# Experts' outputs summed in DRAM by accumulating indirect transfers, and the scatter stage's gate and residual moved into the distance projections

## The reference

```python
g, m = jax.lax.top_k(probs.transpose(0, 2, 1), k)      # k = 128 tokens for each expert
xin = x[batch_idx, m]
h = jax.nn.gelu(jnp.einsum('nekd,edf->nekf', xin, w1), approximate=False)
h = jnp.einsum('nekf,efd->nekd', h, w2)
out = jnp.zeros((n, t, d)).at[batch_idx, m].add(g[..., None] * h)
...
x = x + s * silu(out)                                   # end of the third layer
xn = layernorm(x)                                       # the fourth begins
```

## Time and profile before

| | us |
|---|---|
| three runs, median (lowest to highest) | 3836.95 (3835.36 to 3840.81) |
| the profiled execution | 3840.4 |
| its span | 3838.3 |
| PE busy | 3246.2 (85%) |
| DVE busy | 3057.9 (80%) |
| ACT busy | 2302.0 (60%) |
| POOL busy | 1711.6 (45%) |

### The profile page before, as it was taken

How to read it: one execution, slowest core, us unless ns; L and a number is a source line. 1 busy time by engine, 2 the same in 40 slices (tenths; PEclk the granted TensorE clock), 3 DMA queues, 4 the chain that set the end, 5 groups by cost and what they waited for, 6 DMA issues and landing times. The chain is left out here.

```text
span 3838.3 us, 56660 instructions
## 1 busy us (share of the span) xinstructions
PE 3246.2 (85%) x16737; PEld 1730.1 (45%) x16737; DVE 3057.9 (80%) x4922; ACT 2302.0 (60%) x2769; POOL 1711.6 (45%) x851
## 2 busy tenths in 40 slices
PE   7767988889897997868799999899986977877776
PEld 3322333333236885645434344599985741121111
DVE  6879999999996776856588988577776768888887
ACT  4766666666763334634366666322222759999998
POOL 0009998989983111012200000111134338989996
PEclk9878999999998998977789999999998987888888
DMA  3542333332312356847822333222123642334432
GB/s 126 198 186 118 132 143 144 144 131 108 144 47 92 122 142 167 215 98 243 248 53 77 71 77 75 73 66 66 52 66 111 188 143 95 122 117 126 126 118 83
DMA packets 300300, 465.56 MB, mean 121 GB/s; under 512 B 49687, under 2 KB 242840, under 8 KB 279694
## 3 DMA queue, kind: packets, MB, share of 16 engines
q1 hardware_dynamic: 252670, 404.62, 32.9%
q10 hardware_dynamic: 44432, 51.10, 4.9%
q0 software_dynamic: 3072, 8.39, 0.8%
HBM read 322.48 MB, written 141.33 MB: 121 GB/s over the span
## 5 line engine op out<-in xcount | busy, mean ns | idle before, releaser
L1225 PE MATMUL mamba_psum<-mamba_hc,scan_ident 128*128 128x512 f32 x1024 | 548.8, 644 | 89.8 <-DVE mamba_hc L1133 71.5
L3639 POOL TENSOR_TENSOR distance_dist<-distance_dist,distance_least_all 128x2048 f32<-128x2048 f32 x124 | 558.9, 4537 | 77.4 <-DMA distance_least_all<-distance_least_rows 77.4
L1156 DVE TENSOR_TENSOR_SCAN mamba_psum<-mamba_psum,mamba_drive 128x512 f32<-128x512 f32 x352 | 414.8, 1216 | 22.7 <-issue 10.4
L2726 DVE TENSOR_REDUCE causal_row_max<-causal_psum 128x1 f32<-128x512 f32 x512 | 332.9, 682 | 77.7 <-PE causal_psum L2796 67.7
L1225 PEld LDWEIGHTS mamba_psum<-mamba_hc,scan_ident 128*128 128x128 f32 x1024 | 175.6, 195 | 418.1 <-DVE mamba_hc L1133 255.4
L2685 ACT ACTIVATE causal_probs<-causal_psum 128x1024 f32<-128x1024 f32 x256 | 250.6, 1021 | 122.0 <-PE causal_psum L2819 121.8
L3815 PE MATMUL distance_psum<-distance_shared_k_stacks,distance_shared_q_stacks 102*128 102x512 bf16 x512 | 212.6, 512 | 113.6 <-DVE distance_least L3733 54.3
L3733 DVE TENSOR_REDUCE distance_least<-distance_psum 128x2 f32<-128x1024 f32 x256 | 294.2, 1213 | 9.5 <-PE distance_psum L3815 9.4
L3769 DVE TENSOR_SCALAR distance_dist<-distance_psum 128x1024 f32<-128x1024 f32 x192 | 227.0, 1219 | 82.2 <-PE distance_psum L3830 82.2
L1076 POOL TENSOR_TENSOR mamba_drive<-late_channels,scan_b_all 128x1024 f32<-128x1024 f32 x64 | 149.8, 2354 | 289.4 <-POOLq L32 289.4
L1120 ACT ACTIVATE mamba_psum<-mamba_dt,scan_a_neg 128x512 f32<-128x512 f32 x256 | 167.4, 683 | 140.6 <-DVE mamba_hc L1133 140.2
(11 more groups left out here) (471 smaller groups left out, 8774.5 us busy)
## 6 DMA issues: line engine op xcount, KB each, us to landing
distance_least_all<-distance_least_rows SPq DMA_DIRECT2D x32, 1024.0 KB, 4.6
scan_b_all<-bc SPq DMA_DIRECT2D x16, 1024.0 KB, 4.6
scan_c_all<-bc SPq DMA_DIRECT2D x16, 1024.0 KB, 6.3
mamba_b_all<-bc SPq DMA_DIRECT2D x16, 1024.0 KB, 5.0
mamba_c_all<-bc SPq DMA_DIRECT2D x16, 1024.0 KB, 8.4
choice_w<-L_ffn_w SPq DMA_DIRECT2D x16, 1024.0 KB, 5.5
z<-mamba_in_z SPq DMA_DIRECT2D x8, 1024.0 KB, 3.9
xc<-mamba_in_xc SPq DMA_DIRECT2D x8, 1024.0 KB, 3.9
```

The costliest lines, as they stand in the source:

```text
L1156: dve.tensor_tensor_scan(out, bank, drive[:, n % DRIVES], 0.0, ALU.mult, ALU.add).then_inc(h_ready, 1)
L1225: pe.matmul(ps[:, Y_BANK + m % 2], ident[:, :], hc[:, n % PRODUCTS], start=False, stop=(s == DS - 1)).then_inc(y_summed, 1)
L2726: dve.reduce_max(row_max[:, g % 2, u:u + 1], ps[:, u % 2], AX.X).then_inc(a_max, 1)
L3639: pool.tensor_tensor(dist[:, g % 2, kt], dist[:, g % 2, kt], least_all[:, g % 2], ALU.subtract).then_inc(shifted, 1)
```

## The change

The experts' outputs are no longer kept. Each is added to its token's row in a DRAM array `given2`, by an indirect transfer with `compute_op=ALU.add` that GpSimd starts (`ExpertChoice.scatter`). Eight stores of zeros prepare the array while the causal attention starts. GpSimd's stream in the experts alternates between scatters of the half two before and gathers of the half three ahead. A buffer `o` for each `k` is used again by the next expert, so `outputs` waits for the scatters of the expert before.

The scatter stage is gone. Its transposes of weights stand in steps 3 to 7 of the experts' last half, in seven groups of four that share a bank and one copy on ScalarE, and TensorE waits for the last copy ahead of its last eight parts of the second product. Its gate and residual are `open_gate` (sigmoid on ScalarE) and `combine` (three operations on 128x1024: s times sum, times gate, plus x). In the projections batch 0 is combined by VectorE, the others by GpSimd. SyncE loads `s`, `x` and the sum, two slots deep, and stores the new `x`. The experts' loop now runs from expert 2 to 6, with 0, 1 and 7 written out. The pieces of the diff stand in this order: the helpers and the scatter, the experts' last half (ScalarE, VectorE, TensorE), the zeros, GpSimd's stream in the experts, and the projections (GpSimd, then one line each of ScalarE and VectorE).

```diff
+    def parts_there(self, eng, b, slot):
+        eng.wait_ge(self.parts_loaded[slot], (b - slot) * (self.PARTS * DMA // 2) + self.PARTS * DMA)
+
+    def turn(self, pe, ps, a):
+        if a == 0:
+            pe.wait_ge(self.loaded, self.LOADS * DMA)
+        if a >= 2:
+            pe.wait_ge(self.copied, a - 1)
+        blocks, _, _ = self.groups[a]
+        for n, block in enumerate(blocks):
+            last = pe.transpose(ps[:, self.FIRST_BANK + a % 2, n * P:(n + 1) * P], block, self.ident[:, :])
+        last.then_inc(self.turned, 1)
+
+    def copy(self, act, ps, a):
+        act.wait_ge(self.turned, a + 1)
+        _, dst, scale = self.groups[a]
+        act.mul(dst, ps[:, self.FIRST_BANK + a % 2].rearrange("p (m d) -> p m d", d=D), scale).then_inc(self.copied, 1)
+
+    def open_gate(self, act, b, slot):
+        self.parts_there(act, b, slot)
+        wait_past(act, self.weighed, b * 2)
+        act.activation(self.gate, self.sum[slot], ACT.Sigmoid).then_inc(self.gate_ready, 1)
+
+    def combine(self, eng, b, slot):
+
+        self.parts_there(eng, b, slot)
+        wait_past(eng, self.combined, b)
+        eng.tensor_tensor(self.s[slot], self.s[slot], self.sum[slot], ALU.mult).then_inc(self.weighed, 1)
+        eng.wait_ge(self.gate_ready, b + 1)
+        eng.wait_ge(self.weighed, b * 2 + 1)
+        eng.tensor_tensor(self.s[slot], self.s[slot], self.gate, ALU.mult).then_inc(self.weighed, 1)
+        eng.wait_ge(self.weighed, b * 2 + 2)
+        eng.tensor_tensor(self.x[slot], self.x[slot], self.s[slot], ALU.add).then_inc(self.combined, 1)
+    def store_x(self, sp, x_out, b, slot):
+        sp.wait_ge(self.combined, b + 1)
+        sp.dma_start(token_tiles(x_out, b), self.x[slot]).then_inc(self.x_stored, DMA)
...
+    def scatter(self, pool, distance, e, k):
+
+        sums = self.given.rearrange("b t d -> (b t) d")
+        wait_past(pool, distance.scattered[k], e * (NB // 2) * DMA)
+        for n in range(NB // 2):
+            column = (k * (NB // 2) + n) * NE2 + e
+            pool.indirect_dma_start(
+                out=sums, out_offset=bass.IndirectOffsetOnAxis(ap=self.rows[:, column:column + 1], axis=0),
+                in_=distance.o[:, k, n, :], in_offset=None, compute_op=ALU.add).then_inc(distance.scattered[k], DMA)
 
...
+        WEIGHT_STEPS = {3: (0, 1), 4: (2, 3), 5: (4,), 6: (5,), 7: (6,)}
...
+                        if final and k == 1:
+                            for a in WEIGHT_STEPS.get(f, ()):
+                                distance.copy(act, ps, a)
...
+                    wait_past(dve, distance.scattered[k], e * HB * DMA)
...
+                pe.wait_ge(distance.copied, distance.GROUPS)
                 for f in range(FT2):
                     second_product(NE2 - 1, 1, f)
...
+        sp.wait_ge(self.zeroed, 1)
+        for b in range(NB):
+            sp.dma_start(token_tiles(self.given, b), self.late[:, 0:TT * D].rearrange("p (i d) -> p i d", d=D)).then_inc(
+                self.zeros_stored, DMA)
...
-                for e in range(1, NE2):
-                    for k in range(2):
-                        pool.wait_ge(x_turned, ((e - 1) * 2 + k + 1) * DT)
-                        choice.gather(pool, e, k)
+                def fetch(half):
+                    pool.wait_ge(x_turned, (half - 1) * DT)
+                    choice.gather(pool, half // 2, half % 2)
+
+                def add(half):
+                    pool.wait_ge(o_copied, (half + 1) * HB)
+                    choice.scatter(pool, distance, half // 2, half % 2)
+
+                fetch(2)
+                for half in range(UNITS):
+                    if half >= 2:
+                        add(half - 2)
+                    if half + 3 < UNITS:
+                        fetch(half + 3)
+                add(UNITS - 2)
...
+                choice.scatter(pool, weights, NE2 - 1, 1)
...
+                weights.combine(pool, 1, 1)
+                pool.wait_ge(weights.combined, 2)
...
-                def body(b, slot):
+                def body(b, slot, more):
                     for n in range(split.TILES):
                         split.pool(pool, b, n, slot)
+                    if more and not (isinstance(b, int) and b == NB - 2):
+                        weights.combine(pool, b + 2, slot)
                     pool.wait_ge(norm_middle, b + 1)
                     pool.tensor_tensor(norm_parts[:, 2], norm_rest[:, :], norm_parts[:, 1], ALU.subtract).then_inc(norm_ready, 1)
                     pool.wait_ge(sig_ready, b + 1)
...
+                        weights.open_gate(act, b + 2, slot)
...
+                weights.combine(dve, 0, 0)
```

More of the change, by code:

```diff
@@ L2158, in __init__ @@
         self.mu = c.sb("mu", [P, 2, DT])
[L2159 to L2164, removed]
+        self.loaded, self.turned, self.copied = (c.sem(n) for n in ("loaded", "turned", "copied"))
+        self.scattered, self.parts_loaded = ([c.sem(f"{n}{k}") for k in range(2)] for n in ("scattered", "parts_loaded"))
+        self.gate_ready, self.weighed, self.combined, self.x_stored = (
+            c.sem(n) for n in ("gate_ready", "weighed", "combined", "x_stored"))
+        self.groups = [([self.rows[:, a, n, m * P:(m + 1) * P] for m in range(DT) for n in range(DT)], self.w_t[:, a],
+                        -2.0 if name == "wk" else 1.0) for a, name in enumerate(self.NAMES)]
+        self.groups.append(([self.wo_cols[:, n, gp].rearrange("p h r e -> p (h r e)") for gp in range(GP) for n in range(DT)],
+                            self.wo[:, :, :], 1.0))
     def load_rows(self, sp, names):
@@ new lines, in load_sum @@
+    def load_sum(self, sp, b, slot):
+        sp.wait_ge(self.scattered[b * 2 // NB if isinstance(b, int) else 1], NE2 * (NB // 2) * DMA)
+        sp.dma_start(self.sum[slot], token_tiles(self.given, b)).then_inc(self.parts_loaded[slot], DMA)
+    def parts_there(self, eng, b, slot):
[9 more added lines that the diff above has]
+        last.then_inc(self.turned, 1)
@@ L2666, in _ @@
                 load_next(NB - 2)
+                sp.wait_ge(choice.zeros_stored, NB * DMA)
             @block.gpsimd
@@ L2908, in experts @@
         def experts(eng, body):
-            body(0, False)
-            with eng.Fori(1, NE2 - 1) as e:
+            for e in range(2):
+                body(e, False)
+            with eng.Fori(2, NE2 - 1) as e:
                 body(e, False)
@@ L3065, in body @@
                             turn_x(*following(e, k), TURN_STEPS.index(f))
+                        if final and k == 1:
+                            for a in WEIGHT_STEPS.get(f, ()):
+                                if a == 0:
+                                    pe.wait_ge(o_copied, (UNITS - 2) * HB)
+                                distance.turn(pe, ps, a)
                         first_product(e, k, f)
@@ L3282, in _ @@
                     sp.wait_ge(stored, (NB + 1) * per_batch * DMA)
+                sp.wait_ge(weights.x_stored, NB * DMA)
                 for slot in range(2):
@@ L3311, in body @@
                     pool.tensor_tensor(gate[:, :, :], gate[:, :, :], ffn[:, :, :], ALU.mult).then_inc(gate_ready, 1)
-                with pool.Fori(0, NB // 2) as pair:
-                    for slot in range(2):
-                        body(pair * 2 + slot, slot)
+                in_pairs(pool, body)
             @block.scalar
@@ L3360, in body @@
                     act.activation(gate[:, :, :], ffn[:, :, :], ACT.Sigmoid).then_inc(sig_ready, 1)
+                weights.open_gate(act, 0, 0)
                 ln.act(act, 0)
@@ L3364, in _ @@
                 act.copy(w_parts.high[:, :, :, :], w_t[:, 0:V + 1]).then_inc(w_parts.rounded, 1)
+                weights.open_gate(act, 1, 1)
                 act.wait_ge(filled, FILLS)
```

199 lines of the change are left out of this document (63 added, 136 removed).

## The result

The changed kernel takes 3799.27 us (median of 4 runs, 3796.59 to 3801.68), the kernel before 3836.56 us (3835.36 to 3840.81) on the same chip. The ratio is 0.9895, 95% interval 0.988 to 0.991: faster by 1.05%, where 3794 us was forecast. The profiled execution has a span of 3797.3 us against 3838.3, 41.0 less.

The account below looks back on a forecast made before the run. Scatter stage fully on the path, experts bound by TensorE, projections by a closed 22 us loop through VectorE, TensorE and ScalarE. -94.6 + 5.1 + 4.5 + 42 = -43 us gave 3794 us, range 3765 to 3816.

Parts of the forecast that it names:

- The scatter stage goes: Between experts and projections: 101.7 us go, 7.1 us of stage changes and first combine replace them, 94.6 us saved.
- about 9: Sign expected in the new profile: about 9 us from the experts' last outputs to the projections' first statistics.
- Transposes and tail: Experts' last half: 28 weight transposes cost 3.8 us, TensorE's wait behind the last step 1.3, together 5.1 us.
- Scatter-adds, zeros, loads, sigmoids: Experts, causal attention's start and projections: all hidden, costing nothing; a scatter hides below 5.4 us of the engines.
- Rival A: Experts: accumulating scatters are slow and the experts wait; at 8 us each 166 us lost, 3960 us; chance 0.06.
- D: Rival at the projections' start: the sum arrives 10 us later than assumed, 3804 us; chance inside the main forecast's 0.68.
- First batches: Projections' opening: late gate delays GpSimd's combine, then its memsets to about 40 us, which `rest` awaits; 4.5 us lost.
- Steady batches: Projections: GpSimd's combine collides with VectorE's `mix` and TensorE's clock falls; (5.5 + 1.5) x 6 = 42 us lost.
- rival C: Projections: GpSimd always first and clock falls each batch, 7.2 + 2.5 = 9.7 us x 6, 3812 us; chance 0.12.
- Contention: Steady batches of the projections: GpSimd's three operations delay VectorE's `mix` by 5.5 us a batch.
- the clock: Steady batches of the projections: TensorE at half speed after its idle gap costs 1.5 us a batch, range 0 to 2.
- Rival B: Projections' batches: hardly any contention, 1 us per batch and the clock holds, 6 us lost, 3758 us; chance 0.12.

Follow-up runs that it names:

- 8: Changed kernel with `compute_op=ALU.add` taken from the scatters, so rows are written and not added: ratio 0.9893 to the kernel before.
- 1: Changed kernel without GpSimd's three combine operations in batches 2 to 7, loads, sigmoids and stores kept: ratio 0.9772 to the kernel before.
- 10: Changed kernel, combine behind `xn`, gates a batch ahead, batch 7's at batch 5's start, batch 1's right behind batch 0's: ratio 0.9798 to the kernel before.
- 4: Changed kernel with GpSimd's four memsets of the q stacks' rows put ahead of the combine of batch 1: ratio 0.9902 to the kernel before.
- 11: The changed kernel itself, run again on the chip of the experiments: ratio 0.9893 to the kernel before, 1356.6 us from the experts' first gather to the end.
- 7: Changed kernel with 26 unread matmuls where TensorE waits for VectorE in a batch of the projections: ratio 0.9871 to the kernel before.
- version 9: Changed kernel, combine behind `xn`, gates opened a batch ahead, batch 7's at the start of batch 5's part: ratio 0.9801 to the kernel before.

## Why the prediction was right

*The scatter stage goes, -94.6.* Measured -94.8. The combine ahead of the first statistics took its 5 us (2834.65 to 2839.56), and leaving two stages and entering one took 2.0 (1.9 predicted). The 6.9 us from the last outputs to the first statistics fit the sum's 7.1, not the "about 9" named among the signs.

*Transposes and tail, +5.1.* Measured +4.1 by the books; by the rows 3.0 for the transposes (predicted 3.8; 0.11 us each and not 0.135) and 1.2 for the last copy (1.3).

*Scatter-adds, zeros, loads, sigmoids, nothing.* Right, and shown for the accumulation by 8, for loads and sigmoids by 1. No run isolates the zeros; the stretch that they lie in grew by 2.7 us, within the spread. A scatter takes 1.1 us of the engines against the limit of 5.4. Rival A had nothing to it. D did not happen: VectorE waited 0.74 us for the sum, not 10.

*First batches, +4.5.* Between the first statistics of batches 0 and 1 there are +5.0 us, but not by the step named. The memsets did end 39.4 us into the stage (about 40 predicted), but `rest` no longer waited for them (1.93 us before): from the first statistics to the first `rest` it is 33.7 us against 30.6, +3.1. The delay came ahead of the memsets' end, from the combine of batch 1, by VectorE's rows and GpSimd's:

```profile
2842.10 3.54 DVE L138 TENSOR_SCALAR distance_in_xn<-choice_w,distance_in_ln_moments,distance_in_ln_rstd 128x256 f32<-128x256 f32 x4
...
2854.47 7.47 DVE L3400 TENSOR_SCALAR distance_in_mixed<-distance_in_xn_t,distance_in_mu_not 128x512 f32<-128x512 f32 x4
```

```profile
2842.50 2.34 POOL L2233 TENSOR_TENSOR choice_late<-choice_late 128x1024 f32<-128x1024 f32 x1
2852.71 2.38 POOL L2236 TENSOR_TENSOR choice_late<-choice_late 128x1024 f32<-128x1024 f32 x1 [7.86 <-ACT choice_late L2227]
2855.16 2.44 POOL L2238 TENSOR_TENSOR choice_w<-choice_w,choice_late 128x1024 f32<-128x1024 f32 x1
2857.66 7.88 POOL L3300 MEMSET distance_shared_q_stacks<- 6x2048 bf16 x4
```

`xn` of batch 0 took 1.38 us before, and the scalings 3.30 (3.30 also in 10, where the combine is over by then). Together they lost 6.3 us, and VectorE's wait for ScalarE's root shrank by 1.35 (1.71 to 0.36): +5.0. Moving half of the memsets (4) gained nothing. This step was right by number only.

*Steady batches, +42.* The six intervals grew by 0.6, 7.2, 8.9, 8.8, 8.8 and 7.1, 41.5 us together (44.8 in the second profile, 11). A steady one was mis-sized: 8.8 and not 7.0, nearer to rival C's 9.7. Contention was put at 5.5 and measured 6.3 (7.99 - 1.66; 6.4 by 7); the clock at 1.5 and measured 2.4 to 2.5 (7, and TensorE's 23.51 - 21.04). The clock's was rival C's value, and the contention lay halfway to its 7.2. The mechanism was the one forecast, but the total of 42 is partly luck. Six times 8.8 would have been 53. It came out because not all six intervals are steady ones: the first was long before as well (26.3 us, behind the memsets) and hardly grew, and the last had taken 23.7 with a wait of 1.60 us for `x`. The sum counted all six alike. Rival B was excluded by the trace and by 1.

*What the sum missed.* It gave -43.0 against -41.0. The terms above give -44.2; +0.6 behind the last statistics and +2.7 ahead of the experts make up the rest but 0.1, and the latter is within the spread between executions.

Left open: why each version has its own 748 to 755 us behind the last statistics; and whether the opening, which still has 6 us more than before in version 9 (52.5 against 46.2 for two intervals), could be freed.

## What to carry to other kernels

Work given to an idle GpSimd is priced by what VectorE does in those microseconds, not by GpSimd's idle time: beside scalings from SBUF to SBUF three GpSimd operations of 7.7 us together cost VectorE 6.3 us on the critical path, beside differences that read one array from PSUM nothing. So place it by VectorE's timeline, with a wait if need be (here that, with the sigmoid moved ahead, turned 44 us of cost into 13), look where GpSimd's own later work then falls (the splits, 3.48 us for 1.66 of VectorE's), and price the gap that a collision opens in TensorE's work with the lower clock behind it, 2.4 us for a gap of 7.3.

## What the runs showed that I had not expected

- The same four-operation group suffers equally wherever it is: scalings of `mix` 1.66 to 7.99 us, scalings of `xn` 1.8 to 7.41, beside three GpSimd operations each time. Sums with two inputs in SBUF suffer as well: for batch 1 they took 4.85 us in one profile of the changed kernel and 6.96 in the other, in place of 2.73.
- An accumulating indirect transfer of 128 rows of 1 KB: 1.6 us of issue, 1.1 us of 16 engines, 3.8 us to landing (medians of 64 for the first and last); a plain one 1.1 us, 0.35 us and 2.5 us, with a third of the packets.
- 26 useless matmuls (6.05 us) in a wait of 7.3 us made the kernel 7 to 10 us faster (1346.2 against 1353.2 and 1356.6 to the end).
